# Dummy matmuls left out of the four stages that hold the recurrence of a two-layer decoder kernel

## The chip, the core and the metric

The kernel runs on one NeuronCore of one Trainium2 chip, as one program. The metric is the device time in microseconds (us), median of the runs. TensorE has a clock with two levels, 1.2 and 2.4 GHz; the profile gives the granted share of it, 0.5 for the lower level and 1.0 for the upper.

## The reference

A decoder of two layers runs on x of 16 batches x 512 positions x 256 features in float32; each sublayer is x + f(layernorm(x)).

```
L0: a = sigmoid(xn A^T + bA); b = xn B^T; c, d = sigmoid(xn C^T), sigmoid(xn D^T)
    h = c * scan(h_t = a_t h_(t-1) + d_t b_t);      x += h out^T + b + residual
    x += cross attention over 64 context rows, 16 heads
    x += x W^T + b + (x V_r) C^T
L1: xg = x W_ih^T + b;  for t in 512:  gates = xg_t + h W_hh^T (hidden size 20)
                                       c = sig(f) c + sig(i) tanh(g);  h = sig(o) tanh(c)
    mu_t, sigma_t from h;  w_ji = exp(-(i/(j+1) - mu_j)^2 / 2 sigma_j^2), i <= j, scaled to unit length
    x += w x                                        (position attention, causal)
    x += cross attention with mask and a factor fside on the weights
    x += mixture of 8 experts, one chosen for each position, leaky relu squared
```

What matters here is the loop over t: 512 steps that follow one another, for all 16 batches at once, each with one small matmul. Everything else is ordinary dense work.

## The kernel before

The positions are cut in four chunks of 128, and the batches in four groups of four; a unit is a chunk of a group. The work is laid out in stages 0 to 6. Stages 0 and 1 have two bodies each (two units of layer 0 side by side, on two lanes), stages 2 to 4 four bodies each, stage 5 two, stage 6 one. Stages 1 to 4 hold the recurrence: 128 of its steps in each, 64 per body in stage 1 and 32 per body in stages 2 to 4. Beside it, stages 2 and 3 have a unit of layer 0 and a unit of layer 1, stage 4 a unit of layer 1 and ten tiles of the experts; stage 5 has the last units of layer 1 and experts, stage 6 only experts. The last three bodies of stages 2 to 4 are one loop each.

The order of the instructions is written by a planner when the program is built (`planned_at`, line 391). It has a list of steps for each stream with an engine, an estimated time and what each needs, puts them one by one where they can begin first, and so gets one order for each engine. Steps of the recurrence (stream 2: `gates` on TensorE, `tanh`, `cell`, `tcell`, `state` on ScalarE and VectorE) have first rank but are spread evenly over the body. On the chip each engine goes through its row in order and waits on semaphores; nothing is placed by time.

Behind the planning is a second pass (lines 463 to 472). Where TensorE has, by the plan's own times, nothing to do for more than IDLE = 0.3 us, dummy matmuls (`warm`) are put into its row, one for each 0.22 us of 0.9 times the gap, if the stage stands in WARM. The last condition on line 468 keeps them out of the first body of stage 0, and in the first bodies of later stages before the first `wturn`. Stage 5 is not in WARM. A dummy waits for no semaphore and signals none: it multiplies a 128x512 bf16 tile `warm` by its first 128 columns into a bank that nothing reads at that time. In the trace they are line 1031:

```
    pe.matmul(banks[1][0] if layer > NC_ else px, warm[:, 0:P], warm[:, :], start=True, stop=True)
```

A step of the recurrence is L1023 on TensorE (gates), L1196 and L1197 on ScalarE, L1756, L1758 and L1760 on VectorE, L1200 on ScalarE, L1764 on VectorE (writes `slots`, which the next L1023 waits for). Other names: L946 transposes a normed tile, L1055 the products of layer 0, L952, L963, L989, L1003, L1014 the attention and projections, L1106 and L1112 the position attention, L1162, L1169, L1176 the experts.

Of the kernel before, what the change touches and what calls it, by code (L numbers as in the profile page):

```python
# [378 lines left out]
TILE_LAG = (0.5, 3.0, 8.0, 0.1)  # L379


IDLE, FILL, WARM = 0.3, 0.9, (0, 1, 2, 3, 4, 6)


def planned(stage, rows):
# [1553 lines left out]
```

## Time and profile before

| what | us |
|---|---|
| median of 3 runs | 2477.66 |
| lowest and highest | 2474.67, 2482.07 |
| the profiled execution's own time | 2481.42 |
| its span, first to last instruction | 2479.3 |
| TensorE busy (matmuls) | 2241.2 |
| of it, line 1031 | 450.1 |
| VectorE, ScalarE, GpSimd busy | 1453.5, 1420.2, 794.9 |
| mean granted TensorE clock | 0.958 |

By the first gates of each stage in the trace, stage 1 runs from 310.5 us, stage 2 from 639.8, stage 3 from 1173.3 and stage 4 from 1696.9 to 2093.7; stage 5 ends at 2399 and stage 6 at 2479.3.

In the rows below, PE is TensorE's matmuls, PEld its weight loads, DVE VectorE, ACT ScalarE, POOL GpSimd. Matmuls are pipelined: the ends of records are modelled, and the next can start before the one ahead ends.

### The profile page before, as it was taken

What the parts mean: (1) busy time and instruction counts of PE and PEld (TensorE: products, weight loads), DVE (VectorE), ACT (ScalarE), POOL (GpSimd) and SP (SyncE); (2) the same over time, 40 slices, a digit from 0 to 9 for tenths busy, and PEclk for the clock granted to TensorE, in tenths of its full rate; (3) what the DMA queues carried; (4) which work ended last, traced back from release to release, by engine and by line L of the source; (5) the groups of instructions that cost most, each with busy time, mean ns of one, the idle gap of its engine ahead of it and who ended that gap; (6) DMA issues with size and microseconds to landing.
All of it is one profiled execution on the core that took longest, in us unless ns stands there. A gap on an engine that the chain in (4) does not pass through costs nothing.

```text
span 2479.3 us, 42343 instructions
## 1 busy us (share of the span) xinstructions
PE 2241.2 (90%) x11319; PEld 1477.3 (60%) x11319; DVE 1453.5 (59%) x5504; ACT 1420.2 (57%) x5145; POOL 794.9 (32%) x870
## 2 busy tenths in 40 slices
PE   6979999999999989899999989898888988797987
PEld 3655756556565656566575747465655656575654
DVE  6554576676665657565676766575654646363621
ACT  2634658567484837474665757484664654665722
POOL 2121111201222222222133222223544444574655
PEclk9999999999999999999999999998999999888989
DMA  6030200100303030202021111204333332544323
GB/s 184 28 108 16 62 18 15 49 1 16 93 10 82 1 86 6 75 26 74 26 60 41 50 52 29 80 13 137 103 86 114 99 116 76 158 138 115 91 60 103
DMA packets 237206, 167.09 MB, mean 67 GB/s; under 512 B 97105, under 2 KB 230575, under 8 KB 236990
## 3 DMA queue, kind: packets, MB, share of 16 engines
q1 hardware_dynamic: 222654, 139.51, 20.1%
q0 software_dynamic: 14336, 25.28, 3.5%
q14 instruction: 152, 1.25, 0.2%
q8 instruction: 64, 1.05, 0.2%
HBM read 123.86 MB, written 53.40 MB: 71 GB/s over the span
## 4 chain that ended last, share of the span: by engine, by line
PE 51%; issue 14%; DVE 14%; ACT 8%; POOL 6%; SPq 4%; DMA 2%; DVEq 0%; POOLq 0%; another core or an unknown queue 0%; ACTq 0%
PE p L1055 8%; PE p L1014 6%; PE p L1031 6%; PE p L989 6%; PE p L952 4%; PE p L1003 4%; PE p L963 3%; PE p L946 3%; ACT l_scratch L1248 3%; PE pg L1023 2%; DVE ln_stats L1463 2%; PE p L1112 2%; SPq L788 2%; PE p L986 1%; DVE l_xres L1493 1%
## 5 line engine op out<-in xcount | busy, mean ns | idle before, releaser
L1248 ACT ACTIVATE l_scratch<-p,l_mx 128x64 f32<-128x64 f32 x2048 | 485.5, 324 | 37.2 <-DVE l_mx L1510 25.2
L1031 PE MATMUL p<-warm 128*128 128x512 bf16 x1728 | 450.1, 393 | 0.0
L1816 POOL TENSOR_TENSOR ln_rstd<-ln_ve,neghalf 128x4 f32<-128x4 f32 x96 | 98.4, 1025 | 731.6 <-DVE ln_ve L1472 730.4
L1023 PEld LDWEIGHTS pg<-slots,wcat 128*128 128x128 f32 x1024 | 175.2, 196 | 233.6 <-DVE slots L1764 161.1
L1014 PEld LDWEIGHTS p<-l_vg,l_scratch 128*128 128x128 f32 x2048 | 256.6, 194 | 60.8 <-ACT l_scratch L1256 33.3
L1031 PEld LDWEIGHTS p<-warm 128*128 128x128 bf16 x1728 | 177.5, 107 | 163.7 <-issue 35.3
L1014 PE MATMUL p<-l_vg,l_scratch 128*128 128x34 f32 x2048 | 262.3, 275 | 5.4 <-ACT l_scratch L1256 2.7
L1832 POOL TENSOR_TENSOR l_scratch<-l_scratch,gp 128x512 f32<-128x512 f32 x128 | 162.3, 1270 | 322.4 <-DVE l_sums L1515 321.4
L989 PE MATMUL p<-l_kbd,l_qT 128*128 128x512 f32 x512 | 262.8, 595 | 0.0
L1023 PE MATMUL pg<-slots,wcat 128*128 128x16 f32 x1024 | 178.3, 250 | 75.4 <-DVE slots L1764 54.9
L1510 DVE TENSOR_REDUCE l_mx<-p 128x8 f32<-128x512 f32 x256 | 176.4, 690 | 99.3 <-PE p L989 90.6
L1196 ACT ACTIVATE gates<-pg 96x16 f32<-96x16 f32 x512 | 92.3, 180 | 229.1 <-PE pg L1023 215.3
L1756 DVE SCALAR_TENSOR_TENSOR pg<-gates,pg 20x16 f32<-20x16 f32 x512 | 89.9, 176 | 185.2 <-ACT gates L1196 166.0
L946 PE MATMUL p<-ident,l_xnat 128*128 128x128 f32 x1024 | 155.4, 288 | 44.6 <-ACT l_xnat L1213 40.6
L1256 ACT ACTIVATE l_scratch<-p 128x512 f32<-128x512 f32 x256 | 152.7, 601 | 50.4 <-PE p L1003 42.2
L946 PEld LDWEIGHTS p<-ident,l_xnat 128*128 128x128 f32 x1024 | 122.3, 149 | 88.8 <-ACT l_xnat L1213 47.4
L1003 PE MATMUL p<-ident,l_scratch 128*128 128x128 f32 x1024 | 158.3, 281 | 13.5 <-DVE l_xnat L1525 9.1
L1200 ACT ACTIVATE pg<-pg 20x16 f32<-20x16 f32 x512 | 77.3, 151 | 146.6 <-DVE pg L1760 131.0
L1003 PEld LDWEIGHTS p<-ident,l_scratch 128*128 128x128 f32 x1024 | 119.8, 147 | 65.1 <-issue 41.3
L1764 DVE SCALAR_TENSOR_TENSOR slots<-gates,pg 20x16 f32<-20x16 f32 x528 | 88.8, 171 | 110.2 <-ACT pg L1200 100.0
L1213 ACT ACTIVATE l_xnat<-l_xres,ln_shift,ln_rstd 128x256 f32<-128x256 f32 x160 | 87.2, 593 | 104.2 <-DVE ln_shift L1488 103.9
L1231 ACT ACTIVATE l_xT<-p 128x512 f32<-128x512 f32 x192 | 108.3, 596 | 56.2 <-PE p L946 54.1
(302 smaller groups left out, 4120.1 us busy)
## 6 DMA issues: line engine op xcount, KB each, us to landing
xln<-xln_dram SPq DMA_DIRECT2D x40, 512.0 KB, 3.8
x_dram<-l_xres SPq DMA_DIRECT2D x32, 512.0 KB, 4.1
l_vg<-v_dram SPq DMA_DIRECT2D x30, 544.0 KB
l_kbd<-k_dram SPq DMA_DIRECT2D x512, 16.0 KB
xln_dram<-l_xnat SPq DMA_DIRECT2D x16, 512.0 KB, 3.0
l_xres<-x_dram SPq DMA_DIRECT2D x16, 512.0 KB
x_dram<-l_xnat SPq DMA_DIRECT2D x16, 512.0 KB
xin<-in_x SPq DMA_DIRECT2D x12, 512.0 KB, 3.7
```

Source lines behind the costliest of these rows:

```text
L946: i = pe.transpose(banks[l][m][:, b * P:(b + 1) * P], src[:, b, m * P:(m + 1) * P], ident[:, :])
L989: pe.matmul(banks[l][j], w.qT[:, j, b * P:(b + 1) * P], w.kbd[:, b, j, :, :].rearrange("p a k -> p (a k)"), start=False, stop=True).then_i ...
L1003: i = pe.transpose(t_bank[l][:, p * P:(p + 1) * P], src, ident[:, :])
L1014: i = pe.matmul(o_of(l, layer, c)[:, q * VW:(q + 1) * VW], w.exT[:, j, p, :], w.vg[:, b, q * VW:(q + 1) * VW], start=True, stop=True)
L1023: pe.matmul(pg[:, 0:B], wcat[:, :], slots[:, s % STEPS, :], start=True, stop=True).then_inc(l_pe, 1)
L1031: pe.matmul(banks[1][0] if layer > NC_ else px, warm[:, 0:P], warm[:, :], start=True, stop=True)
L1055: i = pe.matmul(bank, w[:, k, half * P:(half + 1) * P], tiles[lane].xT[:, k, :], start=(k == 0), stop=(k == NH - 1))
L1231: act.activation(w.xT[:, h, :], banks[lane][h], ACT.Identity).then_inc(ln[lane].landed, 1)
L1248: i = act.activation(w.ex[b % 2][:, NE * j + h, :], banks[lane][j][:, h * SK:(h + 1) * SK], ACT.Exp, scale=-1.0, bias=w.mx[:, u % 4, h:h + 1])
L1256: act.activation(w.exT[:, i_ % 2, :, :], t_bank[lane].rearrange("p (a t) -> p a t", a=4), ACT.Identity).then_inc(t.exT, 1)
L1510: dve.tensor_reduce(w.mx[:, u % 4, :], banks[l][j].rearrange("p (a k) -> p a k", a=NE), AX_X, ALU.min).then_inc(t.top, 1)
L1832: pool.tensor_tensor(ex, ex, gp[lane][:, b:b + 1, :].broadcast_to([P, NE, SK]), ALU.mult).then_inc(t.gated, 1)
```

## The change

```diff
-IDLE, FILL, WARM = 0.3, 0.9, (0, 1, 2, 3, 4, 6)
+IDLE, FILL, WARM = 0.3, 0.9, (0, 6)
 
 def planned(stage, rows):
```

WARM is read in the second pass alone, behind the planning, so the order of all other steps is the same on each engine. The rows of dummies leave TensorE's row in stages 1 to 4. Executed, they are 142 in each of the 2 bodies of stage 1; 111 and 3 x 115 in stage 2; 75 and 3 x 80 in stage 3; 63 and 3 x 113 in stage 4: 284 + 456 + 315 + 402 = 1457 of 1728. The 95 of stage 0 and the 176 of stage 6 stay.

TensorE at the start of a body of stage 1 (`-` before, `+` now; L1023 are the first steps of the recurrence, L946 the transposes of the first norm):

```order
-L1031 MATMUL p<-warm 128x512 x2
-L1023 MATMUL pg<-slots,wcat 128x16
-L1031 MATMUL p<-warm 128x512 x14
-L1023 MATMUL pg<-slots,wcat 128x16
-L1031 MATMUL p<-warm 128x512 x11
-L1023 MATMUL pg<-slots,wcat 128x16
-L1031 MATMUL p<-warm 128x512 x8
-L946 MATMUL p<-ident,l_xnat 128x128 x8
-L1023 MATMUL pg<-slots,wcat 128x16
-L1031 MATMUL p<-warm 128x512 x5
+L1023 MATMUL pg<-slots,wcat 128x16 x3
+L946 MATMUL p<-ident,l_xnat 128x128 x8
```

The 40 dummies between the steps are gone, and the steps stand in the same order.

TensorE near the start of a body in the loop of stage 2, between a turn of position weights (L1106), a step of the recurrence and the first products of layer 0 (L1055):

```order
 L1106 MATMUL p<-ident,l_scratch 128x128 x4
-L1031 MATMUL p<-warm 128x512 x7
 L1022 REGISTER_ALU
 L1023 MATMUL pg<-slots,wcat 128x16
 L1036 ISA
 L946 MATMUL p<-ident,l_xnat 128x128 x8
-L1031 MATMUL p<-warm 128x512 x10
 L1044 ISA
 L1055 MATMUL p<-l_xT,wD 128x512
```

Here 7 stood ahead of a step of the recurrence, and 10 between a transpose and the products that need its result.

## Rows read from the trace of the kernel before

**Rows 1.** The page: granted clock in 40 slices, the chain's shares, dummies' matmuls
```profile
PEclk9999999999999999999999999998999999888989
...
PE 51%; issue 14%; DVE 14%; ACT 8%; POOL 6%; SPq 4%; DMA 2%; DVEq 0%; POOLq 0%; another core or an unknown queue 0%; ACTq 0%
...
L1031 PE MATMUL p<-warm 128*128 128x512 bf16 x1728 | 450.1, 393 | 0.0
```

**Rows 2.** Busy time by stretch (from:to, length, engines, clock, DMA): stages 1 to 5
```profile
310.50:639.80 329.30, 318.13 (x1554) 197.13 (x1554) 227.52 (x953) 207.36 (x796) 54.84 (x49) 1.00 0.10 28
639.80:1173.30 533.50, 501.09 (x2563) 326.94 (x2563) 332.93 (x1276) 321.35 (x1206) 138.20 (x121) 0.97 0.18 46
1173.30:1696.90 523.60, 486.70 (x2472) 320.92 (x2472) 346.38 (x1273) 327.71 (x1210) 137.97 (x121) 0.96 0.18 50
1696.90:2093.70 396.80, 346.06 (x1887) 232.47 (x1888) 226.48 (x938) 227.02 (x916) 182.33 (x241) 0.95 0.36 103
2093.70:2399.00 305.30, 252.27 (x1333) 192.80 (x1331) 137.11 (x434) 174.22 (x548) 182.94 (x235) 0.87 0.40 112
```

**Rows 3.** The same stretches, line 1031 alone (PE, PEld, clock, DMA)
```profile
310.50:639.80 329.30, 70.33 (x282) 28.45 (x282) 1.00 0.10 28
639.80:1173.30 533.50, 116.54 (x456) 47.00 (x456) 0.97 0.18 46
1173.30:1696.90 523.60, 86.94 (x315) 33.10 (x315) 0.96 0.18 50
1696.90:2093.70 396.80, 105.60 (x395) 41.18 (x395) 0.95 0.36 103
```

**Rows 4.** The chain of waits by line, in stages 1, 2, 3 and 4
```profile
by line: PE p L1055 14.4%; PE p L1014 6.6%; PE p L952 6.4%; PE p L1031 6.3%; PE p L989 5.7%; PE pg L1023 5.4%; SPq L788 4.5%; issue 4.1%; DVE ln_stats L1463 3.8%; PE p L1003 3.7%; PE p L946 3.5%; DVE l_xres L1493 3.2%; PE p L963 3.0%; DVE s
...
by line: issue 15.4%; PE p L1055 10.1%; ACT l_scratch L1248 6.8%; PE p L1031 5.9%; PE p L1014 5.4%; PE p L952 5.0%; PE p L963 4.9%; PE p L989 4.8%; PE p L946 4.2%; DVE ln_stats L1463 3.3%; PE p L1003 3.2%; POOL id_dram L1841 2.4%; ACT l_scr
...
by line: issue 19.2%; PE p L1055 7.6%; PE p L1014 7.5%; PE p L989 6.9%; PE p L952 5.1%; PE p L1003 4.5%; ACT l_scratch L1248 3.9%; PE p L963 3.6%; PE p L946 3.3%; PE pg L1023 3.1%; PE p L1031 2.8%; PE p L1112 2.8%; DVE ln_stats L1463 2.4%; 
...
by line: issue 19.7%; PE p L1031 7.3%; PE pg L1023 4.1%; PE p L1014 4.0%; DMA xln<-xln_dram 4.0%; PE p L1112 3.9%; SPq L788 3.8%; PE p L989 3.7%; POOL out L1868 3.0%; PE p L1003 2.9%; POOL id_dram L1841 2.4%; PE p L963 2.2%; PE p L1176 2.0%
```

**Rows 5.** Timeline (start, length, engine, line), stage 1, ten dummies before a step
```profile
467.69 2.32 PE L1031 MATMUL p<-warm 128*128 128x512 bf16 x10
...
469.80 0.17 DVE L1764 SCALAR_TENSOR_TENSOR slots<-gates,pg 20x16 f32<-20x16 f32 x1
470.02 0.30 PEld L1023 LDWEIGHTS pg<-slots,wcat 128*128 128x128 f32 x2 [0.51 <-DVE slots L1764]
```

**Rows 6.** Timeline, stage 2, seven dummies before a step
```profile
916.06 3.19 PE L1031 MATMUL p<-warm 128*128 128x512 bf16 x7
...
916.84 0.17 DVE L1764 SCALAR_TENSOR_TENSOR slots<-gates,pg 20x16 f32<-20x16 f32 x1
...
919.05 0.45 PE L1023 MATMUL pg<-slots,wcat 128*128 128x16 f32 x2
```

**Rows 7.** Busy time by stretch (columns of rows 2): with dummies, without, without
```profile
310.50:320.50 10.00, 8.87 (x47) 4.62 (x47) 8.06 (x38) 5.08 (x16) 6.04 (x6) 1.00 0.09 26
...
2100.70:2112.90 12.20, 4.57 (x35) 3.96 (x36) 4.01 (x21) 5.70 (x11) 1.62 (x4) 0.67 0.23 65
...
643.80:654.00 10.20, 7.77 (x20) 4.73 (x21) 3.77 (x20) 6.00 (x19) 2.67 (x2) 0.50 0.23 73
```

**Rows 8.** TensorE by form, 643.9 to 654 us (busy us, mean ns)
```profile
L1055 PE MATMUL p<-l_xT,wD 128*128 128x512 f32 x4 | 3.8, 1100 | 0.9 <-ACT l_xT L1231 0.9
L946 PE MATMUL p<-ident,l_xnat 128*128 128x128 f32 x8 | 2.2, 428 | 0.2 <-ACT l_xnat L1213 0.2
```

**Rows 9.** TensorE by form, 790 to 865 us
```profile
L946 PE MATMUL p<-ident,l_xnat 128*128 128x128 f32 x22 | 3.4, 280 | 0.6 <-ACT l_xnat L1213 0.6
...
L1055 PE MATMUL p<-l_xT,wD 128*128 128x512 f32 x5 | 2.5, 592 | 0.0
```

**Rows 10.** Timeline, TensorE, the same four products at either clock
```profile
649.47 3.78 PE L1055 MATMUL p<-l_xT,wD 128*128 128x512 f32 x4 [0.93 <-ACT l_xT L1231]
...
793.60 1.88 PE L1055 MATMUL p<-l_xT,wA 128*128 128x512 f32 x4
```

## The prediction

> **What bounds the kernel now.** I read the page first. TensorE is what the end depends on most: the chain that ended last is on it for 51% of the span, and the granted clock stands in the top tenth in nearly all slices, lower only toward the end [rows 1]. Next I put the stages side by side [rows 2]: stages 1 to 4, which lose their dummies, have clocks of 1.00, 0.97, 0.96 and 0.95; stage 5, which never had any, has 0.87. Then line 1031 alone in those stretches [rows 3], its share of the chain [rows 4], and the places where dummies stand ahead of real work [rows 5, 6]. Last I looked at what work costs at the lower clock [rows 7 to 10]. With a clock c, the share of time at 1.2 GHz is 2(1 - c), so stage 5 spends 26% of its time there and stages 1 to 4 together (0 + 32 + 42 + 40) / 1783 us = 6.4%.
>
> **What is removed, and what that gives back.** 1457 dummies go; nothing is added or moved. In the rows they are busy for 70 + 117 + 87 + 106 = 380 us [rows 3]. That isn't the gain. A dummy costs time only if the real instruction behind it could have started earlier. The chain puts 6.3%, 5.9%, 2.8% and 7.3% of the four stages on line 1031 [rows 4]: 21 + 31 + 15 + 29 = 96 us. This is the upper end, and too high, since the chain follows the engine's row where a modelled end overhangs the release. In rows 5 ten dummies fill a wait: `slots` is written at 469.97 and the step's weight load starts at 470.02, no later than it would without them. In rows 6 the clock is at 1.2 GHz, seven dummies last 3 us, `slots` is ready at 917.01 and the step starts at 919.05: 2.0 us lost, though a recurrence that is late by itself is only sometimes what the end of the body waits for. Lower end of the gain: 0. I found the first kind far more often than the second and take a fifth of 96, 20 us. What is late next in the first kind is what the dummies covered: the norm's transposes wait for ScalarE and VectorE, the gates for `slots`.
>
> **What the dummies held up: the clock.** From 310.5 to 320.5 us TensorE has 47 matmul records, of which 33 are dummies (the 14, 11 and 8 of the first piece of the order), and the clock is 1.00. From 2100.7 to 2112.9, in stage 5, it has 35 small records, no dummy, then a wait; the clock falls to 0.67. From 643.8 to 654.0, behind a thin stretch of the first body of stage 2 where the planner's condition keeps dummies out, it is 0.50 [rows 7]. So thin stretches do take the clock down in this kernel, also with the recurrence running in them.
>
> How much time will newly be at 1.2 GHz? The trace of before does not show it, so from both sides. Lower end: stages 1 to 4 come to stage 5's rate, 0.26 x 1783 = 464 us, less the 114 us they have, 350 us. Upper end by idle time: take line 1031 out of TensorE's busy time, and the idle time is 82 + 149 + 124 + 156 = 511 us in stages 1 to 4 and some 55 us in stage 5 (which has 79 us at the low clock, 1.44 us for each idle one); that gives 735, less 114 = 620 us. Taking a run's modelled busy time out whole overstates idle time, and much idle time lies in short waits between dense work; against that, stage 4 is thinner than stage 5. I take 430 us, nearer to stage 5's rate. The mean clock of stages 1 to 4 would be 1 - (114 + 430) / 1783 / 2 = 0.85.
>
> What does a microsecond at the low clock cost? The same four products take 1.88 us at 2.4 GHz and 3.78 us at 1.2 [rows 10]; single records go from 592 to 1100 ns and a transpose from 280 to 428 [rows 8, 9]. The engine does half of what it would, so a low microsecond in which the chain is on TensorE costs half a microsecond, and one in which the chain is on another engine costs nothing. The chain's TensorE share without dummies is 51 - 6 = 45% over the span [rows 1, 4]. At the low clock this share of work, taking twice as long, fills 0.90 / 1.45 = 62% of the time; but the low stretches lie where real work waits for others, so it is less there. Ends 0.3 and 0.7; I take 0.5. Cost: 430 x 0.5 / 2 = 107 us.
>
> [...] No row here shows a low stretch of which all is on the chain.
>
> Sum: 107 - 20 = +87 us. On the profiled execution (2481.4 us, 2.1 over its span) that gives 2568; on the median of the runs, 3.7 us lower, 2565. The bounds: a small cost with a large gain, 350 x 0.4 / 2 - 45 = +25, is 2503; a large cost, 620 x 0.5 / 2 - 5 = +150, is 2628.
>
> Edits that cost nothing: VectorE, ScalarE, GpSimd and the DMA queues keep their rows; a dummy signals nothing, so no wait changes; stages 0, 5 and 6 keep theirs. The weight loads of dummies (150 us, [rows 3]) lie between the same matmuls and go with them. The first real weight load behind a gap was not held by them, as rows 5 show.
>
> **Rivals.**
>
> *A, faster: the rows are in the way.* The dummies are sized by the plan's times, not the chip's; if many runs are like rows 6, the recurrence gets its step earlier each time, and stages 2 to 4 shorten as long as real work alone keeps the clock up. For it: 5.9% and 7.3% of the chain, and TensorE's work without dummies still fills some three quarters of stages 1 to 3. Against it: stage 5, with 82% real work, lost 26% of its time to the low clock. Price: half of the 96 us given back, some 15 us lost (60 us low, at 0.5 / 2): -33, 2445. It decides if less than about 190 us become low (190 x 0.5 / 2 = 48).
>
> *B, no change: the low time lies beside the chain.* The clock falls, but where the chain sits on ScalarE, VectorE, POOL or a transfer, and "issue" (15 to 20% of stages 2 to 4, [rows 4]) hides no TensorE work: 350 x 0.15 / 2 = 26 less 20, +6, and 2484 or less. Against it: bursts of TensorE work follow directly on the waits, as the products at 649.47 do on a wait for ScalarE [rows 10], and those bursts are what runs slow. [...]
>
> *C, much slower: the low clock holds itself.* [...] For it: after 643.8 the clock stayed down for 10 us though there was work [rows 7]. Against it: in stage 5 it recovered each time, with 0.87 in the mean.
>
> That the change does something else than it says is no rival: the order of real instructions on TensorE is the same, as the two pieces of the order show.
>
> **Chances.** The forecast 0.78, A 0.07, B 0.08, C 0.07. A measurement of this kernel can tell about 0.3%, 7 us, from no change. Slower by more: the forecast, C and a little of B, 0.87; the same: most of B, 0.06; faster: A, 0.07. The range 2503 to 2628 takes the bounds of the unknown costs and leaves out A, B's centre and C.
>
> **What would show it.** In the profile after: line 1031 x271; the clock of stages 1 to 4 at 0.85, with 1.00 lost in stage 1; stages 5 and 6 as long as before (305 and 80 us); the means of L1055, L1014 and L1023 up, as more of their records are at 1.2 GHz. Each stage should grow, stages 2 to 4 the most. A mean clock of 0.93 or more in stages 1 to 4 would say that I overrate the fall, and leave A or B. A clock of 0.85 with equal time would say that the chain was elsewhere (B). Stages that got shorter by 10 us or more at equal clock would say that I took the dummies' own cost too low. A clock below 0.80 would be C.

## The result and the profile after

| | before | after |
|---|---|---|
| median of 4 runs, us | 2476.16 | 2614.86 |
| lowest, highest | 2472.24, 2482.07 | 2609.84, 2625.43 |
| profiled execution: own time, span | 2481.42, 2479.3 | 2625.43, 2623.5 |
| mean granted TensorE clock | 0.958 | 0.842 |

The changed kernel is slower: ratio 1.056, 95% interval 1.0531 to 1.059, 139 us. That lies in the range of 2503 to 2628; the forecast of 2565 was 50 us too low, so the forecast loss of 87 us is 63% of the measured one.

The page after, for [rows 1]: TensorE's busy time, the granted clock in 40 slices, the chain (the work that ended last, followed back from wait to wait), and two lines whose means rose. Columns of the last two are busy us, mean ns, idle time ahead and what ended most of it.

```profile
PE 2144.5 (82%) x9862; PEld 1523.0 (58%) x9862; DVE 1453.0 (55%) x5504; ACT 1422.2 (54%) x5145; POOL 793.6 (30%) x870
...
PEclk9989999797786969788788989697877768698989
...
PE 5%; POOL 3%; issue 2%; ACT 1%; DVE 1%; DMA 1%; SPq 1%; POOLq 0%; ACTq 0%; DVEq 0%
...
L1023 PE MATMUL pg<-slots,wcat 128*128 128x16 f32 x1024 | 201.6, 274 | 203.8 <-DVE slots L1764 189.6
...
L946 PE MATMUL p<-ident,l_xnat 128*128 128x128 f32 x1024 | 200.7, 348 | 96.2 <-ACT l_xnat L1213 90.3
```

The same two lines of the page before:

```profile
L1023 PE MATMUL pg<-slots,wcat 128*128 128x16 f32 x1024 | 178.3, 250 | 75.4 <-DVE slots L1764 54.9
...
L946 PE MATMUL p<-ident,l_xnat 128*128 128x128 f32 x1024 | 155.4, 288 | 44.6 <-ACT l_xnat L1213 40.6
```

The clock line is where to look: in [rows 1] it is 9 in nearly all slices, here the slices from the eighth on move between 6 and 9. VectorE, ScalarE and POOL were busy as long as before, within 2 us each. TensorE has 1457 matmul records fewer and is busy only 97 us less, though 380 us of dummies went [rows 3]. The chain of this trace breaks off early (its shares add up to 14%), so it can't be used for the comparison; stretches can.

Busy time by stretch, stages 1 to 5, for [rows 2] (from:to, length, then busy us and count of PE, PEld, DVE, ACT and POOL, the clock, the DMA share and GB/s):

```profile
314.10:679.00 364.90, 301.60 (x1272) 205.56 (x1272) 227.16 (x953) 207.92 (x796) 54.34 (x49) 0.84 0.10 29
679.00:1259.90 580.90, 469.39 (x2108) 338.72 (x2108) 332.34 (x1276) 321.26 (x1206) 138.37 (x121) 0.81 0.17 40
1259.90:1823.20 563.30, 465.96 (x2156) 333.08 (x2156) 345.00 (x1270) 328.22 (x1210) 138.07 (x121) 0.85 0.17 46
1823.20:2248.70 425.50, 319.99 (x1501) 247.78 (x1500) 228.35 (x942) 229.24 (x920) 181.67 (x240) 0.75 0.33 96
2248.70:2545.00 296.30, 245.89 (x1313) 188.30 (x1314) 136.10 (x431) 172.30 (x544) 180.10 (x232) 0.88 0.41 115
```

The record of the granted clock has shares of 1.00 and 0.50 and no other in all twelve traces of this study, so the low time of a stretch ("low" below) is 2(1 - clock) x length. The dummies show what the two levels do. In the trace of before their starts within a run lie 216 ns apart at 1.00 and 427 ns at 0.50 (medians), with records of 379 and 634 ns: 512 columns at 2.37 and at 1.20 columns in a nanosecond. These are the levels that are called 2.4 and 1.2 GHz ahead of the result. In us:

| stage | length before, after | difference | low before, after | difference per newly low us |
|---|---|---|---|---|
| 1 | 329.3, 364.9 | +35.6 | 0, 117 | 0.30 |
| 2 | 533.5, 580.9 | +47.4 | 32, 221 | 0.25 |
| 3 | 523.6, 563.3 | +39.7 | 42, 169 | 0.31 |
| 4 | 396.8, 425.5 | +28.7 | 40, 213 | 0.17 |
| together | 1783.2, 1934.6 | +151.4 | 114, 720 | 0.25 |

These low times come from clocks of two digits, so they are good to a few us. The clock's record in the two traces, added up exactly, has 0, 27, 41 and 41 us low before and 116, 222, 174 and 216 after: 109 and 728, of which 619 us are new. The prices per newly low us are then 0.31, 0.24, 0.30 and 0.16.

The rest of the span, stages 0, 5 and 6, is 7 us shorter; stage 5 alone went from 305 to 296 us. From the last step of the recurrence to the end it took 371 to 385 us in the traces of all other kernels of this study and 389 in the one of before, so that is no effect of the change.

How a loss arises is seen at the first body of stage 1. After:

```profile
314.08 0.40 PE L1023 MATMUL pg<-slots,wcat 128*128 128x16 f32 x2 [1.22 <-POOL slots L1796]
316.76 0.61 PE L1023 MATMUL pg<-slots,wcat 128*128 128x16 f32 x2 [2.28 <-DVE slots L1764]
319.71 0.61 PE L1023 MATMUL pg<-slots,wcat 128*128 128x16 f32 x2 [2.34 <-DVE slots L1764]
321.78 1.97 PE L946 MATMUL p<-ident,l_xnat 128*128 128x128 f32 x8 [1.46 <-ACT l_xnat L1213]
323.85 0.61 PE L1023 MATMUL pg<-slots,wcat 128*128 128x16 f32 x2
325.53 2.08 PE L1055 MATMUL p<-l_xT,wD 128*128 128x512 f32 x2 [1.07 <-ACT l_xT L1231]
```

The same place before:

```profile
310.47 0.40 PE L1023 MATMUL pg<-slots,wcat 128*128 128x16 f32 x2 [0.79 <-POOL slots L1796]
...
318.33 1.04 PE L946 MATMUL p<-ident,l_xnat 128*128 128x128 f32 x8
...
321.97 1.13 PE L1055 MATMUL p<-l_xT,wD 128*128 128x512 f32 x2
```

With 38 dummies between them, the first step and the first product lay 11.50 us apart; without, 11.45. That isn't yet the dummies' own cost, since the clock falls in between: its record has it low from 316.0 to 329.7 us. The second step comes 2.68 us behind the first, mostly still at the full clock; with 14 dummies between them it came 3.26 us behind, so there the dummies did hold it, by 0.6 us. What follows loses that again at the low clock. The eight transposes take 1.97 us and not 1.04, two products 2.08 us and not 1.13. The places of the dummies are plain idle time now, ended by VectorE and ScalarE.

That the low time is longer than I counted has a form that can be seen: a clock that fell stays down longer than before. In the clock's record it falls 18 times in stages 1 to 4 before, 6.1 us long in the mean, and 63 times after, 12.0 us in the mean. The longest stretch after, and one at the turn to the second body of stage 2:

```profile
2231.00:2275.20 44.20, 30.98 (x123) 25.15 (x122) 13.51 (x67) 18.92 (x54) 16.11 (x23) 0.50 0.30 88
821.20:845.00 23.80, 14.41 (x37) 8.60 (x38) 9.33 (x44) 12.75 (x41) 7.87 (x9) 0.50 0.56 88
```

TensorE is busy there for 31 of 44 us and 14 of 24 us, all of it at a granted clock of 0.50.

### The profile page after: what moved, and what is told of

It reads as the page before. It is cut to its first block and busy times, and to the rows that moved or that the text cites. A ratio compares the mean times of both kernels' runs of the same rounds, so it can differ in the third digit from the quotient of the medians.

```text
span 2623.5 us, 39420 instructions
## 1 busy us (share of the span) xinstructions
PE 2144.5 (82%) x9862; PEld 1523.0 (58%) x9862; DVE 1453.0 (55%) x5504; ACT 1422.2 (54%) x5145; POOL 793.6 (30%) x870
## 5 line engine op out<-in xcount | busy, mean ns | idle before, releaser
L1023 PEld LDWEIGHTS pg<-slots,wcat 128*128 128x128 f32 x1024 | 201.0, 226 | 357.0 <-DVE slots L1764 276.3
L1023 PE MATMUL pg<-slots,wcat 128*128 128x16 f32 x1024 | 201.6, 274 | 203.8 <-DVE slots L1764 189.6
L1014 PEld LDWEIGHTS p<-l_vg,l_scratch 128*128 128x128 f32 x2048 | 280.7, 209 | 63.4 <-ACT l_scratch L1256 37.7
L1014 PE MATMUL p<-l_vg,l_scratch 128*128 128x34 f32 x2048 | 283.4, 288 | 10.9 <-ACT l_scratch L1256 10.1
L946 PE MATMUL p<-ident,l_xnat 128*128 128x128 f32 x1024 | 200.7, 348 | 96.2 <-ACT l_xnat L1213 90.3
L946 PEld LDWEIGHTS p<-ident,l_xnat 128*128 128x128 f32 x1024 | 162.3, 186 | 132.2 <-ACT l_xnat L1213 88.3
L1003 PE MATMUL p<-ident,l_scratch 128*128 128x128 f32 x1024 | 170.5, 297 | 28.6 <-DVE l_xnat L1525 15.4
L1003 PEld LDWEIGHTS p<-ident,l_scratch 128*128 128x128 f32 x1024 | 130.4, 158 | 73.7 <-issue 44.7
L952 PE MATMUL p<-wO,l_xT 128*128 128x256 f32 x512 | 141.9, 428 | 7.9 <-ACT l_xT L1235 7.9
L963 PE MATMUL p<-l_xT,wQ 128*128 128x512 f32 x256 | 139.5, 650 | 5.1 <-ACT l_xT L1231 4.9
```

The lines of the kernel that those rows point to most:

```text
L946: i = pe.transpose(banks[l][m][:, b * P:(b + 1) * P], src[:, b, m * P:(m + 1) * P], ident[:, :])
L952: i = pe.matmul(pairs[l][:, b * D:(b + 1) * D], x[:, k, b * P:(b + 1) * P], w[:, k, :], start=(k == 0), stop=(k == NH - 1))
L963: i = pe.matmul(banks[l][2 - half], wQ[layer][:, k, half * P:(half + 1) * P], w.xT[:, k, :], start=(k == 0), stop=(k == NH - 1))
L1003: i = pe.transpose(t_bank[l][:, p * P:(p + 1) * P], src, ident[:, :])
L1014: i = pe.matmul(o_of(l, layer, c)[:, q * VW:(q + 1) * VW], w.exT[:, j, p, :], w.vg[:, b, q * VW:(q + 1) * VW], start=True, stop=True)
L1023: pe.matmul(pg[:, 0:B], wcat[:, :], slots[:, s % STEPS, :], start=True, stop=True).then_inc(l_pe, 1)
```

## The experiments

All ratios are to runs of the kernel before on the same chip.

**Dummies of 16 columns (e1_thin).**

```diff
-pe.matmul(banks[1][0] if layer > NC_ else px, warm[:, 0:P], warm[:, :], start=True, stop=True)
+cols = 16 if 1 <= layer <= NC_ else NT
+pe.matmul((banks[1][0] if layer > NC_ else px)[:, 0:cols], warm[:, 0:P], warm[:, 0:cols], start=True, stop=True)
```

> All 1457 dummies of stages 1 to 4 stand where they stood, but each has 16 columns in place of 512. Theory (the clock falls because TensorE's array is idle, and the loss is work at 1.2 GHz): the clock of the span is near the changed kernel's 0.842 and the time is 2600 to 2640 us, since the thin dummies hold next to nothing up. Rival (it is enough that TensorE has instructions, weight loads among them, in its row): the clock stays near 0.95 and the time near 2476 us or 10 to 25 us below, as thin dummies are in nobody's way.

Measured: 2622.34 us, ratio 1.060 (1.0554 to 1.0648), clock 0.843. Stages 1 and 2 of this kernel (line 1032 has the dummies):

```profile
L1032 PE MATMUL p<-warm 128*128 128x16 bf16 (+1 forms) x1716 | 150.2, 206 | 0.8 <-issue 0.2
...
311.50:682.90 371.40, 315.73 (x1555) 221.08 (x1555) 227.20 (x953) 207.94 (x796) 54.45 (x49) 0.82 0.10 29
682.90:1261.80 578.90, 479.77 (x2564) 353.75 (x2564) 332.49 (x1276) 321.22 (x1206) 138.27 (x121) 0.82 0.16 40
```

This is what the theory said. All weight loads of the dummies are there (1728 in the trace; 12 of their matmul records are missing), and the time and the clock are those of the changed kernel. So their instructions and weight loads alone don't hold the clock: with 512 columns each it is 0.958, with 16 it is 0.843. Sizes between were not run, and what it is in the columns that holds the clock isn't shown. It also says that the loss is not something the shorter program does by itself.

**Fewer, and half as many again (e2_half, e3_more).** By rounding down in each gap, the factor of 0.5 leaves 660 of the 1457 dummies, which is 45%; 1.5 makes 2253 of them.

```diff
-range(int(gap * FILL / 0.22))
+range(int(gap * (FILL * LESS if 1 <= stage <= NC_ else FILL) / 0.22))    # LESS = 0.5, LESS = 1.5
```

> Half as many dummies in every gap of stages 1 to 4 (660 in place of 1457). Theory: about half of the low time comes back, clock 0.88 to 0.92, time 2520 to 2570 us. Rival (the dummies that stand in the way cost most, and half of them hold the clock as well as all): clock 0.94 or more, 2450 to 2475 us.

> 1.5 times as many dummies per gap in stages 1 to 4 (2253), more than the planned gaps hold. Theory: the clock can hardly rise (0.958 to about 0.97), and the dummies' own cost shows by itself: if 1457 of them cost 20 us on the chain, these cost that and most of the excess, 796 x 0.216 us = 172 us of engine time of which a quarter to a half lands on the chain: 2510 to 2560 us. Rival (dummies cost nothing, only the clock counts): 2460 to 2476 us.

Measured: half, 2529.81 us, ratio 1.0237 (1.0195 to 1.0278), clock 0.909. More, 2526.68 us, ratio 1.0234 (1.0193 to 1.0275), clock 0.966. Both as the theory said. With 660 left, 260 us are newly low by the clock's record, not 619, and the loss is 58 us, not 139. Stages 1 and 2 with more:

```profile
312.00:656.00 344.00, 338.79 (x1688) 215.23 (x1713) 226.75 (x953) 207.67 (x796) 54.94 (x49) 1.00 0.11 30
656.00:1209.80 553.80, 540.01 (x2771) 352.04 (x2811) 332.46 (x1276) 322.20 (x1206) 137.94 (x121) 0.98 0.17 43
```

Stage 1 tells the dummies' own price by itself, since its clock is 1.00 here as in [rows 2]: 159 more dummies, 14.7 us more, 0.09 us each, where each occupies TensorE for 0.216 us (from the ten of [rows 5]: 2.32 us less a record of 0.379, over nine). Over all, 796 more cost 56 us, 0.07 each, with a little less low time than before. These are dummies beyond the planned gaps, though, so their price is not that of the first 1457.

**Long gaps only, short gaps only (e4_long, e9_short).**

```diff
-if gap > IDLE and stage in WARM
+if gap > (LONG if 1 <= stage <= NC_ else IDLE) and stage in WARM              # e4_long, LONG = 1.2
+if IDLE < gap <= (LONG if 1 <= stage <= NC_ else 99.0) and stage in WARM      # e9_short, LONG = 1.2
```

> Dummies in stages 1 to 4 only in planned gaps over 1.2 us (1108 in place of 1457). Theory: the short runs hold up little of the clock and are often in the way, so the long ones keep most of it: clock 0.93 to 0.95, 2470 to 2500 us. Rival (every dummy counts alike for the clock): a quarter of the 139 us is lost, 2511 us.

> The complement of the run with long gaps only: in stages 1 to 4 dummies stand only in planned gaps of 0.3 to 1.2 us (349 of 1457). In the trace after the change the clock fell 63 times in these stages, not 18, and stayed down for 12.0 us in the mean, not 6.1. Theory (a fallen clock holds itself down, since work at half speed leaves TensorE's neighbours waiting; a few dummies between short pieces of work bring it back): falls about as many as after, 55 to 65, but shorter, 8 to 10 us, and more than the dummies' share of the loss is won back: 2540 to 2565 us. Rival (every dummy counts alike, 24% of them win back 24% of 139 us): 2570 to 2580 us. Second rival (short runs matter only where long ones keep the clock up): 2600 to 2615 us.

Measured: long, 2511.5 us, ratio 1.0151 (1.0105 to 1.0197), clock 0.933; short, 2562.87 us, ratio 1.0398 (1.0361 to 1.0434), clock 0.874. The first is the rival's number: the 349 short-gap dummies are worth some 37 us, and mine, that they are in the way, is wrong. The second by its absolute time is in my theory's interval, but the kernel before ran at 2461.74 us beside it, so the difference, +98 us, is the rival's; the two losses, 1.5% and 4.0%, add up to nearly the change's 5.6%. What my theory said of the clock did come: 61 falls of 9.2 us in the mean, against 63 of 12.0 without any, so in these traces the short runs don't prevent falls and do end them sooner.

The sum hides that the stages differ. Long only, stages 1 and 2; then short only, the same:

```profile
313.80:644.20 330.40, 312.13 (x1502) 195.42 (x1516) 227.60 (x953) 207.36 (x796) 54.87 (x49) 0.99 0.10 29
644.20:1206.10 561.90, 509.29 (x2439) 345.70 (x2455) 332.92 (x1276) 321.31 (x1206) 138.06 (x121) 0.91 0.17 43
```

```profile
312.60:683.50 370.90, 314.41 (x1310) 214.97 (x1310) 227.12 (x953) 208.12 (x796) 54.35 (x49) 0.82 0.10 29
683.50:1240.20 556.70, 461.82 (x2215) 318.70 (x2215) 332.42 (x1276) 321.85 (x1206) 138.06 (x121) 0.87 0.17 42
```

In stage 1 the long gaps hold everything: 330.4 us with them alone, 370.9 with the short ones alone, against 329.3 with both. In stage 2, 561.9 and 556.7 against 533.5: either kind alone saves only about half of the 47 us. Bounded by the steps in the same way, stage 3 takes 525.0 us with the long gaps alone and 557.3 with the short ones alone, against 523.6 with both and 563.3 with none; stage 4 takes 401.2 and 403.4, against 396.8 and 425.5. So long gaps do nearly all in stages 1 and 3, and either kind does most of the work in stage 4. The short-gap dummies are 14%, 24%, 27% and 28% of those of the four stages and win back nothing, 51%, 15% and 77% of the stages' losses. So that every dummy counts alike comes out in the sum and in none of the stages, and the sum's agreement looks like chance.

**One stage at a time (e5_off1, e6_off4).**

```diff
-IDLE, FILL, WARM = 0.3, 0.9, (0, 1, 2, 3, 4, 6)
+IDLE, FILL, WARM = 0.3, 0.9, (0, 2, 3, 4, 6)     # e5_off1
+IDLE, FILL, WARM = 0.3, 0.9, (0, 1, 2, 3, 6)     # e6_off4
```

> Only the 284 dummies of stage 1 go. In the trace after the change, stage 1 was 36 us longer at 116 us more low clock. If the stages add up, 2505 to 2515 us, and the other stages as long as before. Rival (a stage's loss is made good or made worse by the next, whose work starts from what it leaves): another time than 2500 to 2520, with stages 2 to 4 changed by 5 us or more.

> Only the 402 dummies of stage 4 go, the stage where TensorE has least to do and where the low clock went up most per microsecond (41 to 212 us of some 400), but the stage grew by only 28 us. If the price of low time is set by the chain's share on TensorE, which is least here, 2500 to 2510 us at 170 us more low time: 0.17 us each, against 0.31 in stage 1. Rival (one price everywhere, 0.23): 2515 us or more.

Measured: without stage 1's, 2498.86 us, ratio 1.0139 (1.0111 to 1.0167), 34 us; without stage 4's, 2494.83, ratio 1.0118 (1.0093 to 1.0142), 29 us. In absolute time both are below what I wrote, as the kernel before ran at 2462.68 us beside them; as differences they are close to the 36 and 28.7 us of the table. Stages 1 and 2 without stage 1's, then stage 4 without its own (this window ends 3.4 us too early; up to the same place behind the last step as in the table, stage 4 is 425.4 us long):

```profile
312.10:676.70 364.60, 301.29 (x1273) 205.51 (x1273) 227.12 (x953) 207.91 (x796) 54.43 (x49) 0.84 0.10 30
676.70:1209.40 532.70, 500.38 (x2564) 326.35 (x2564) 332.94 (x1276) 321.31 (x1206) 138.15 (x121) 0.97 0.17 44
```

```profile
1696.10:2118.10 422.00, 319.40 (x1492) 248.22 (x1493) 225.83 (x932) 227.99 (x913) 179.74 (x239) 0.74 0.33 97
```

Stage 1 alone is as long as in the changed kernel (364.9), stage 2 behind it as before (533.5), and stage 4 alone as in the changed kernel (425.5). The losses stay in their stages, and the table's lines can be read one by one, though not to the microsecond: stage 4 of e5_off1, which kept its dummies, took 387.3 us, some 10 less than before. The rival of e5_off1 had named 5 us or more in another stage as its sign, and this one trace has them, but the whole time lost, 34 us, agrees with stage 1's own loss. Stage 4 pays least for its low time, 0.17 against 0.30, and the 29 us of e6_off4's medians say the same. That fits the chain, whose real TensorE lines in [rows 4], as far as they are listed, add up to 49%, 38%, 44% and 23% of stages 1 to 4, where the prices are 0.30, 0.25, 0.31 and 0.17. No run varied the chain's share by itself.

**Runs that stand in the way, cut (e7_trim, e8_tail, e10_best).** In the trace of before some runs of dummies end after the next real instruction was released, as in [rows 6]. A table TRIM of planned runs sets these to fewer or none. The main lines of the edit:

```diff
+TRIM = {(4, False, 6): 0, (4, False, 19): 0}     # e8_tail: (stage, first body, number of the run): left
-kept += [("pe", 3, "warm", i) for i in range(int(gap * FILL / 0.22))]
+count = int(gap * FILL / 0.22)
+run += count > 0
+kept += [("pe", 3, "warm", i) for i in range(TRIM.get((stage, rows, run), count) if count else 0)]
```

> The dummies stay, but 22 runs of them in stages 1 to 4 (planned) that the trace of before showed ending after the next real instruction was released are cut to end before it or taken out: 1457 less some 240. Theory (what dummies cost is the real instructions that they hold, some 50 us in all over the stages, of which a part is on the chain; the cut runs hardly hold up the clock): 2445 to 2470 us, faster than before. Rival (they are needed as much as the others: clock down by 0.01 to 0.02): 2475 to 2495 us.

> Only two of those runs in the loop of stage 4 go, 16 ahead of the transpose of an expert tile at the end of a body, which started 3.6 us after its data, and 4 ahead of the first one. Theory: 3 bodies x 3.6 us are in the way, but the next matmul waits for ScalarE in any case: 2460 to 2475 us. Rival (the wait behind them is where the clock falls, and without the 16 it falls earlier): 2475 to 2490 us.

> The kernel before with nine planned runs of dummies cut or taken out in stages 1, 3 and 4 and at a body's start in stage 2, where the clock did not fall in the run with 22 cut: 112 fewer. Theory (each holds a step of the recurrence or an expert's transpose by 0.4 to 3.6 us, without which the clock stays): 0.2 to 0.6% faster than before, 2450 to 2465 us at a clock of 0.955 to 0.965. Rival (what they hold isn't on the chain, as in the run with 22 cut): within 0.2% of before.

Measured: e7_trim, 22 planned runs, by the trace 186 dummies fewer (not some 240), 2465.59 us, ratio 1.0005 (0.9987 to 1.0024). e8_tail, 60 fewer, 2457.89 us, ratio 0.9977 (0.9961 to 0.9993). e10_best, 103 fewer in its trace (not 112), 2460.62 us, ratio 0.998 (0.9954 to 1.0007). The clocks of the profiled executions are 0.954, 0.963 and 0.961, but the medians over all executions tell more: 0.951, 0.958 and 0.958, against 0.959 before.

The theory of e7_trim, faster, is wrong, and so is its rival's time. Its stage 2:

```profile
641.30:1177.50 536.20, 494.32 (x2504) 325.03 (x2504) 332.93 (x1276) 320.41 (x1206) 138.06 (x121) 0.96 0.18 46
```

It is 2.7 us longer than in [rows 2], with 41 us low and not 27 by the clock's record. Over all executions a clock lower by 0.008 is 39 us more of low time, which at 0.25 each would cost 10 us; so the cut dummies may have given back about as much, by this estimate, and the clock took it. The run shows only the sum, nothing. e8_tail came as its theory said, a few us less than before: the 16 dummies at the end of stage 4's bodies and the 4 ahead of its first expert tile are too many, by some 6 us in 2463, beyond the interval but just so, and in one of three such kernels. With that e8_tail has the lowest median here; e10_best, which holds the same two cuts and seven more, doesn't differ from it or clearly from before. Its 0.2% lies at the edge of both its theory and its rival and decides nothing.

## Why the prediction came out as it did

*What bounds it.* Right. The clock of stages 1 to 4 set by the dummies was the loss: e1_thin takes only their columns away and gets all of it.

*What the dummies' going gives back (20 us).* Not settled, and probably too high. e7_trim took out those that visibly held something and gained nothing in sum, by the estimate above some 10 us that the clock took back; with e8_tail there are 6 us to show. The step's weak part was "a fifth of 96": in part the chain's 96 us were modelled ends overhanging a release, as in [rows 5], and no row said how large a part. No run takes dummies away at an unchanged clock all over stages 1 to 4, so the gain can't be told from the price of a low microsecond. If it is near 6 us, the forecast was 14 us too fast by this step.

*How much time becomes low (430 us, bounds 350 and 620).* This is the term that was mis-sized. It was 606 us by the table and 619 by the clock's record, at the upper bound, and mean clock 0.81 in place of 0.85 (720 / 1934.6 / 2 = 0.19). At 0.25 each the missing 189 us are 47 us of loss, nearly all of the 52 by which the forecast fell short. I took stage 5's low share of the time as the nearer row. But stage 5 is the wrong neighbour for that: its real work is denser, 83% of the time by [rows 2], where stages 1 to 4 have 61 to 76% without dummies. The count by idle time, which I had taken for an overstatement, was the better one: 1.44 low us for each of the 82, 149, 124 and 156 idle us gives 118, 215, 179 and 225 us, and the record has 116, 222, 174 and 216. Part of that is luck. Stage 5's idle time is 53 us and not 55, so its rate was 1.50 and the bound 650 us; and over the idle time that the changed kernel itself shows (63, 112, 97 and 106 us) the rates are 1.8 to 2.0, so two errors cancel. And low stretches didn't only get more, they got twice as long, 12.0 us for 6.1. I had that as rival C, as something all or nothing; it came in part. What keeps a fallen clock down wasn't tried by itself; with the short-gap dummies of e9_short the stretches are 9.2 us.

*What a low microsecond costs (0.25).* Right as far as it can be told: these are net prices, in which whatever the dummies' going gives back is already taken off. Over stages 1 to 4 151.4 / 606 = 0.25; over the whole, by the medians, 139 / 606 = 0.23. With a gain of 20 us inside, the stages' price would be 0.28. By stage it goes from 0.17 to 0.31. With the measured low time my sum would have been 606 x 0.25 - 20 = 132 us, and with an own cost of nothing 152; 139 lies between. The products of [rows 10] take 3.78 us for 1.88, so TensorE itself loses half of the low time, 303 us of the 606. The measured 139 are about half of that, which fits an end that waited for TensorE in about half of the low time; this was not measured by itself.

*The rivals.* A, faster, and B, no change, are out: the low time was far above the 190 us under which A decides, and enough of it lay on the chain to cost 0.25 us each. C, with 0.9 of the low time on the chain, comes to 430 x 0.9 / 2 - 20 = +174, 2652, above what was measured, but its low clock that holds itself is in part what was seen, with low stretches of 12.0 us for 6.1, and made the loss larger than forecast.

*What would show it.* Line 1031 x271, all of stages 1 to 4 longer, the means of L1014 (275 to 288 ns), L1023 and L1055 (in stage 2 its first products, 663 to 855 ns) up: all came. Stage 6 is as before within 2 us; stage 5 is 9 us shorter, in a trace whose stretch behind the last step is as long as in those of the other kernels. "Stages 2 to 4 the most" holds for 2 and 3; stage 4 grew least, as its price per low microsecond is the lowest. A clock under 0.80 for C: stage 4 alone is there, with 0.75.

## What to carry to other kernels

Where TensorE waits often, judge dummy matmuls by the clock of each stretch and not by their busy time or their share of the chain: 380 us of busy dummies saved 139 us here, their own cost taken off. Take the new low time from a stretch whose real work is as thin as the one in question, or from idle time and not from the share of the whole; count with low stretches that grow longer (from 6.1 to 12.0 us here); and multiply by the share of the low time in which the chain is on TensorE, halved. That share was estimated here; what was measured is their product, 0.25 us for a newly low one over stages 1 to 4. Dummies of 16 columns in place of 512 did nothing in this kernel (2622 us at a clock of 0.843), so their size isn't free to choose; their number can go down where they stand beyond the gap and the end waits for what they hold, which was worth some 6 us.

## What the runs showed that I had not expected

1457 dummies of 16 columns, with as many weight loads of 128x128 as before, held nothing: clock 0.843 against 0.842 without any. And which dummies matter depends on the stage: 40 in short gaps of stage 1 are worth nothing (370.9 us with them, 364.9 without any, one trace each), while in stage 2 the 108 in short gaps are worth 24 of 47 us.
